# Inverting 16-row triangular blocks: row-by-row substitution against 4x4 blocks joined to 8 and to 16 rows, in the delta-rule stage of a one-core Trainium2 kernel

## The reference, cut to what matters

```python
def step(M, kvq):
    k_t, v_t, q_t = kvq
    out_t = jnp.einsum('bhdk,bhk->bhd', M, q_t)
    kn = k_t / (jnp.linalg.norm(k_t, axis=-1, keepdims=True) + 1e-06)
    pred = jnp.einsum('bhdk,bhk->bhd', M, kn)
    surprise = pred - v_t
    coef = pred + lr[None, :, None] * surprise
    M_new = M - jnp.einsum('bhd,bhk->bhdk', coef, kn)
    return (M_new, out_t)
M_final, outs = jax.lax.scan(step, M0, (k_s, v_s, q_s))
```

## Time and profile before

| what | value |
|---|---|
| median of 3 runs | 1468.79 us (1467.89 to 1471.7) |
| the profiled execution's own time | 1469.33 us |
| its span, first to last instruction | 1467.5 us |
| what lies around the span | 1.8 us |
| mean granted TensorE clock | 0.936 of full speed |
| instructions on DVE | 2568, of them 960 in the inversion (L1270 and L1274, 480 each) |
| busy time of the inversion on DVE | 144.0 us (L1270) and 113.5 us (L1274) |
| the last step's end | POOL and PE lead the chain of waits with 31% and 34% of the span |

### The profile page before, as it was taken

How to read it: one execution, slowest core, us unless ns; L and a number is a source line. 1 busy time by engine, 2 the same in 40 slices (tenths; PEclk the granted TensorE clock), 3 DMA queues, 4 the chain that set the end, 5 groups by cost and what they waited for, 6 DMA issues and landing times.

```text
span 1467.5 us, 45643 instructions
## 1 busy us (share of the span) xinstructions
PE 1253.4 (85%) x17572; PEld 1019.9 (69%) x17572; DVE 870.9 (59%) x2568; ACT 625.4 (43%) x1539; POOL 596.7 (41%) x721
## 2 busy tenths in 40 slices
PE   3889999999994779889888988898889888988764
PEld 3756666666663668778777877787778777877763
DVE  0163433333333377768777777677767777777661
ACT  0012222222221455555555655555555555555431
POOL 0000000000002474566566656665666566556521
PEclk9989999999995789999999999999999999999886
DMA  8769999999940011111111111111111111111110
GB/s 308 266 229 384 374 366 380 376 368 376 375 156 17 3 26 19 30 25 28 23 29 24 27 24 30 24 27 24 29 24 27 23 29 26 25 21 26 24 18 17
DMA packets 176413, 169.84 MB, mean 116 GB/s; under 512 B 118198, under 2 KB 146425, under 8 KB 175609
## 3 DMA queue, kind: packets, MB, share of 16 engines
q1 hardware_dynamic: 176234, 167.37, 35.0%
HBM read 154.72 MB, written 12.58 MB: 114 GB/s over the span
## 4 chain that ended last, share of the span: by engine, by line
PE 34%; POOL 31%; issue 22%; DVE 8%; ACT 2%; DMA 1%; SPq 1%; POOLq 0%; DVEq 0%; ACTq 0%
PE PS L434 29%; POOL region L1092 11%; POOL region L1073 4%; POOL region L1078 3%; POOL xr_lo L1097 2%; POOL region L1086 2%; POOL region L1049 1%; POOL region L1084 1%; PE PS L503 1%; POOL region L1068 1%; POOL region L1063 1%; POOL region L1056 1%; PE PS L673 1%; POOL region L1040 1%; DVE region L1410 1%
## 5 line engine op out<-in xcount | busy, mean ns | idle before, releaser
L434 PE MATMUL PS<-region 64*64 64x64 f32 (+5 forms) x5936 | 366.5, 287 | 44.5 <-DMA region<-in_w 23.0
L434 PEld LDWEIGHTS PS<-region 64*64 64x64 f32 (+3 forms) x5936 | 243.9, 140 | 144.2 <-issue 102.8
L1092 POOL TENSOR_TENSOR region<-region,powers 128x24 f32<-128x24 f32 x64 | 215.2, 3362 | 5.0
L1019 POOL TENSOR_TENSOR region<-region,powers 128x1 f32<-128x1 f32 x32 | 6.1, 189 | 417.1 <-DVE region L1200 417.1
L1280 DVE TENSOR_REDUCE region<-region 128x12 f32<-128x768 f32 x96 | 91.0, 948 | 129.7 <-ACT region L894 129.5
L683 PE MATMUL PS<-region 64*64 64x64 f32 x4608 | 165.1, 228 | 2.4 <-ACT region L922 2.1
L683 PEld LDWEIGHTS PS<-region 64*64 64x64 f32 x4608 | 151.9, 142 | 21.2 <-issue 17.3
L1270 DVE TENSOR_TENSOR region<-region 96x1 f32<-96x1 f32 (+14 forms) x480 | 144.0, 300 | 24.9 <-DMA region<-n_scratch 10.3
L434 PE MATMUL PS<-cw_hi,xr_hi 128*128 128x512 f32 (+3 forms) x384 | 146.8, 382 | 10.0 <-POOL xr_lo L1097 10.0
L434 PE MATMUL PS<-cw_lo,xr_hi 128*128 128x512 f32 (+3 forms) x384 | 138.9, 362 | 0.0
L434 PE MATMUL PS<-cw_hi,xr_lo 128*128 128x512 f32 (+3 forms) x384 | 137.5, 358 | 0.0
(11 more groups left out here) (165 smaller groups left out, 2179.8 us busy)
## 6 DMA issues: line engine op xcount, KB each, us to landing
region<-in_Wq SPq DMA_DIRECT2D x32, 1152.0 KB, 5.6
region<-in_Wk SPq DMA_DIRECT2D x32, 1152.0 KB, 8.0
region<-in_Wv SPq DMA_DIRECT2D x32, 1152.0 KB, 7.6
region<-in_x SPq DMA_DIRECT2D x32, 384.0 KB, 6.6
region<-in_w SPq DMA_DIRECT2D x3, 2304.0 KB, 11.8
region<-h_scratch SPq DMA_DIRECT2D x64, 96.0 KB, 1.9
n_scratch<-region SPq DMA_DIRECT2D x256, 12.0 KB, 1.6
region<-i_scratch SPq DMA_DIRECT2D x256, 12.0 KB, 1.8
```

Of the source, the lines that this page charges most:

```text
L434: return nc.tensor.matmul(dst, lhsT, rhs, start=first, stop=last)
L1092: pool.tensor_tensor(rs[:, cols], rs_var[:, cols], root[:, cols], ALU.pow).then_inc(S["rs_ready"], 1)
```

## The change: what it does

The 16x16 blocks are inverted in three levels instead of row by row. `invert_small` does rows 1 to 3 of all four 4x4 diagonal blocks of each 16x16 block together, with the same multiply and reduce, on access patterns with one more dimension (three multiplies and three reduces). `join(k, 4, 3)` makes two 8x8 inverses out of four 4x4 ones: two multiplies of 64 elements, one reduce of 128 elements to 32 (into the new buffer `mid`), two multiplies of 64, two reduces of 64 to 16. `join(k, 8, 5)` makes the 16x16 inverse out of two 8x8 ones: a multiply of 512 elements, a reduce of 512 to 64, a multiply of 512, a reduce of 512 to 64. The second multiply of each join reads `inv` down its columns: neighbouring elements of that operand lie 16 words apart. Between dependent instructions a semaphore wait stands as before.

In DVE's order `invert_small` and the join of 4 stand where rows 1 to 7 stood, and the join of 8 stands where rows 8 to 15 stood. `prod` grows from 256 to 512 elements a partition and `mid` adds 64. The new function `invert(k)` at the end of the first hunk of code is called by nothing.

```diff
--- before.py
+++ after.py
@@ -246,7 +246,8 @@
         dT = part("second", P, HEADS, SEQ)
         blocks = part("second", NBLK * HEADS, BLK, BLK)
         inv = part("second", NBLK * HEADS, BLK, BLK)
-        prod = part("second", NBLK * HEADS, BLK, BLK)
+        prod = part("second", NBLK * HEADS, 512)
+        mid = part("second", NBLK * HEADS, 64)
         eT = part("second", P, HEADS, SEQ)
         y, c1, z, c = [part("second", P, KD) for _ in range(4)]
         outT = part("second", P, HH, P)
@@ -1259,20 +1260,56 @@
                 dve.tensor_tensor(wo[:, :, :], wo[:, :, :], lr[:, HEADS:].unsqueeze(2).to_broadcast([P, HH, ATT]), ALU.mult)\
                    .then_inc(S["fold_ready"], 1)
 
-            def invert(k, rows):
-
-                if rows[0] == 1:
-                    dve.wait_ge(S["gather_done"], (k + 1) * 16)
-                    need(dve, "inv_stored", k * 16)
-                for r in rows:
+            def diag(buf, at, *dims):
+
+                return bass.AP(buf.tensor, buf.offset + at, [buf.ap[0]] + [list(n) for n in dims])
+
+            def invert_small(k):
+
+                dve.wait_ge(S["gather_done"], (k + 1) * 16)
+                need(dve, "inv_stored", k * 16)
+                for r in range(1, 4):
                     if r > 1:
-                        dve.wait_ge(S["sub_step"], k * (BLK - 2) + r - 1)
-                    dve.tensor_tensor(prod[:, 0:r, 0:r], inv[:, 0:r, 0:r],
-                                      blocks[:, r, 0:r].unsqueeze(1).to_broadcast([NBLK * HEADS, r, r]), ALU.mult)\
-                       .then_inc(S["sub_mul"], 1)
-                    dve.wait_ge(S["sub_mul"], k * (BLK - 1) + r)
-                    last = dve.tensor_reduce(inv[:, 0:r, r], prod[:, 0:r, 0:r], AX, ALU.add)
-                    last.then_inc(S["sub_step" if r < BLK - 1 else "d_ready"], 1)
+                        dve.wait_ge(S["sub_step"], 6 * k + r - 1)
+                    step = BLK * 4 + 4
+                    dve.tensor_tensor(diag(prod, 0, (r * r, 4), (r, r), (1, r)), diag(inv, 0, (step, 4), (BLK, r), (1, r)),
+                                      diag(blocks, r * BLK, (step, 4), (0, r), (1, r)), ALU.mult).then_inc(S["sub_mul"], 1)
+                    dve.wait_ge(S["sub_mul"], 7 * k + r)
+                    dve.tensor_reduce(diag(inv, r, (step, 4), (BLK, r)), diag(prod, 0, (r * r, 4), (r, r), (1, r)), AX, ALU.add)\
+                       .then_inc(S["sub_step"], 1)
+
+            def join(k, size, done):
+
+                pairs = BLK // (2 * size)
+                low = size * BLK
+                step = 2 * (low + size)
+                plane = size * size
+                cube = (plane, size), (size, size), (1, size)
+                dve.wait_ge(S["sub_step"], 6 * k + done)
+                for p in range(pairs):
+                    last = dve.tensor_tensor(diag(prod, p * plane * size, *cube),
+                                             diag(blocks, p * step + low, (0, size), (BLK, size), (1, size)),
+                                             diag(inv, p * step, (BLK, size), (0, size), (1, size)), ALU.mult)
+                last.then_inc(S["sub_mul"], 1)
+                dve.wait_ge(S["sub_mul"], 7 * k + done + 1)
+                dve.tensor_reduce(diag(mid, 0, (1, pairs * plane)), diag(prod, 0, (size, pairs * plane), (1, size)),
+                                  AX, ALU.add).then_inc(S["sub_step"], 1)
+                dve.wait_ge(S["sub_step"], 6 * k + done + 1)
+                for p in range(pairs):
+                    last = dve.tensor_tensor(diag(prod, p * plane * size, *cube),
+                                             diag(mid, p * plane, (size, size), (0, size), (1, size)),
+                                             diag(inv, p * step + low + size, (0, size), (1, size), (BLK, size)), ALU.mult)
+                last.then_inc(S["sub_mul"], 1)
+                dve.wait_ge(S["sub_mul"], 7 * k + done + 2)
+                for p in range(pairs):
+                    last = dve.tensor_reduce(diag(inv, p * step + size, (BLK, size), (1, size)),
+                                             diag(prod, p * plane * size, *cube), AX, ALU.add)
+                return last
+
+            def invert(k):
+                invert_small(k)
+                join(k, 4, 3).then_inc(S["sub_step"], 1)
+                join(k, 8, 5).then_inc(S["d_ready"], 1)
 
             def moments(t, m):
                 dve.wait_ge(S["sq_ready"], 3 * t + m + 1)
@@ -1420,7 +1457,7 @@
                 if live(m):
                     ffn_out(m)
                 if live(k):
-                    invert(k, range(8, BLK))
+                    join(k, 8, 5).then_inc(S["d_ready"], 1)
                 if live(l):
                     gate_and_add(l)
                 if live(x + 1):
@@ -1459,7 +1496,8 @@
                 if live(x + 1):
                     normalise(x + 1)
                 if live(j):
-                    invert(j, range(1, 8))
+                    invert_small(j)
+                    join(j, 4, 3).then_inc(S["sub_step"], 1)
                 if live(t):
                     scale(t, 2)
```

## The result

The changed kernel takes 1401.74 us (median of 4 runs, 1393.09 to 1409.35) against 1468.34 us (4 runs) of the kernel before, a ratio of 0.9534 with a 95% interval of 0.9501 to 0.9567. That is 67 us less; the forecast was 1407 us, 62 us less. The profiled execution took 1401.61 us for a span of 1399.8 us.

A forecast was written before the change was run, and what follows sets the result against it. The prediction took DVE's 29.04 us loop through take_norm as the bound, not PE; 2.37 - 0.5 + 0.07 = 1.94 us a period over 31 periods, plus 1.9 us at the end, gave 1407 us, 8-in-10 range 1382 to 1434 us.

The forecast's parts named there:

- The bound: DVE's loop from take_norm to take_norm, 29.04 us, sets the period, with all of the inversion, 9.09 us, on it.
- The second half: Rows 8 to 15: four instructions in 2.80 us against 5.17, saving 2.37 us a tile before the column cost.
- The column reads: Second multiply of each join, hopping 16 words: 1.0 ns an element, 0.5 us in the second half, 0.13 in the first.
- the row L1147: Existing six-element instruction with two streams hopping 193 words, read as 1.4 ns an element and used to price column reads.
- The first half: Rows 1 to 7, 14 instructions become 13: 0.07 us saved a period, between -0.5 and +0.5.
- two meetings with L1097: POOL's L1097 starting 1.55 or 1.20 us into the first half: ends at 3.4 (0.5 saved) or 3.7 us (0.1 lost).
- The sum: A period: 2.37 - 0.5 + 0.07 = 1.94 us saved, 29.04 to 27.10; 62 us in all, 1407 us.
- the rival with free columns: Joins' column reads cost nothing: 2.57 us a period, 1387 us; chance 0.15, shared with a better meeting with L1097.
- Dear columns: Joins' column reads cost 1.4 to 2.8 ns an element: 1416 to 1444 us; chance 0.14 (beyond 1425).
- Short runs: Joins' runs of 4 and 8 elements cost 8 ns each: period 0.5 us longer, 1485 us; chance 0.04 (slower).
- PE taking over: PE's loop, 25.4 us, 27.2 with lower clock, bounds: 1411 us, or 1468; chance 0.05 that it or another wait takes nearly all.
- fixed to `take_norm`: The gather's load and its landing before the inversion keep their time behind take_norm, so neither saving touches them.

The follow-up runs named there:

- e5: Changed kernel with take_norm moved up on DVE behind gate_and_add, norm_h2 moved back, and key_lengths ahead of residual_rstd on POOL: 1369.21 us, ratio 0.9359.
- e1: First half of the change alone, rows 8 to 15 one by one as in the kernel before: 1463.75 us, ratio 0.9964, commonest period 28.55 us.
- e3: Changed kernel with the second multiply of both joins reading inv along rows, so the result isn't the inverse: 1378.49 us, ratio 0.9385.
- e2: Changed kernel with both 8x8 diagonal blocks by substitution, two at once, then the join of 8: 1409.13 us, ratio 0.9587.
- e6: Changed kernel with right_side and high_part moved ahead of moments(t, 2), into DVE's wait for ACT: 1387.35 us, ratio 0.9472.
- e4: Changed kernel, same inverse, with the joins' second multiply reading rows and the reduce after it reading prod with a hop: 1400.52 us, ratio 0.9526.
- e8: Changed kernel with GpSimd's low_part (L1098) cut to 128x64 elements from the second tile on, so the output is another: 1365.72 us, ratio 0.9317.
- e9: Changed kernel with the moves of e5 and e6 together: 1366.39 us, ratio 0.9312.
- e10: e9 with POOL's low_part also moved ahead of input_rstds: 1350.53 us, ratio 0.9188.
- e7: Changed kernel with PE's gates(x) placed ahead of start_y(k), in its wait for take_e: 1395.41 us, ratio 0.9504.

## Why the prediction was right, point by point

*The bound.* Right in the main: the period repeats through `take_norm` (e5), and the second half of the inversion lies on the loop whole (e1, e3). After the change every stretch but the two halves kept its length (11.71, 4.48, 1.13, 2.64). But the sentence that all 30 instructions of the inversion lie on the loop is too broad. The stretch from `take_norm` through `take_e`, `start_y`, ACT's squares and DVE to the join of 4 has POOL's way to L1098 beside it, and POOL's ends last (e2, e6): of the first half only what is left behind L1098's end counts. The forecast's own sum for the first half had this right, since it let L1097 keep its time behind `take_norm`.

*The second half.* Forecast 2.80 us and 0.5 for the columns, 3.30; measured 3.12. The interpolated 699 and 682 ns were 677 and 682. The column reads were over-priced: 0.377 us instead of 0.5, as the row L1147, with its two hopping streams, gave too much for one. The estimate from the Trainium skill, "Vector Engine (DVE) Microarchitecture Reference", section 5.2 (0.35 to 0.74 us), holds the measured value at its lower end. e3 shows that the order of the words makes the difference; that pairs of adjacent words are what counts, as the page has it, no run here shows. e4 bears on a remark there, that a one-source read alternating between two regions ran at full rate: a reduce reading with a constant hop of 8 words didn't.

*The first half.* The forecast worked out two meetings with L1097, with ends at 3.4 and 3.7 us, and took a value between them less 0.13 for columns. Both were measured, 3.43 and 3.77; the commonest is the better one, 0.49 us saved where I took 0.07.

*The sum.* The two terms together were under-sized: the commonest period fell by 2.54 us, not 1.94, 0.60 us or 19 us over 31 periods. That the time came out within 5 us of the forecast all the same is luck: the mean lies 0.49 us above the commonest period (15 us over 31), against 0.07 before, and no step of mine had this term. With all periods at 26.50 the time would have been about 1387 us, the value of the rival with free columns, though the columns aren't free. Part of the term is the clock: the seven falls behind `start_y` hold 10.0 of the 15.2 us. But falls at this place are in seven periods of the kernel before as well, and those exceed 29.04 by only 2.9 us together. What differs most is the meeting with L1098. Before, a late start of the inversion made the first half shorter: in the seven periods DVE's wait for ACT's squares is 4.8 us longer in sum, and the halves are 2.4 us shorter (3.55 to 3.70 us each in place of 3.92). After, the wait is 6.8 us longer and six of the seven halves are 3.76 to 3.78 us in place of 3.43, 2.0 us longer in sum. In four more periods, with no fall, the inversion starts only 0.2 to 0.3 us late, and each is about 0.6 us longer. With a short L1098 (e8) the half never exceeds 2.83 us.

*The rivals.* Free columns: out, by the 1054 ns. Dear columns: out, 0.74 ns an element is below 1.4. Short runs: 677 ns for 64 runs of 8 leaves nothing for a run. PE taking over: in one inner period of the changed kernel (from 857.93, 26.87 us, with a fall of the clock `take_norm` starts 0.04 us after PE's key norms), not in the others; but its loop of 25.4 us, worked out for it, is what e5, e9 and e10 stop at (25.45). The gather isn't fixed to `take_norm`, as the forecast called it: its blocks land 15.0 to 16.9 us after it in the inner periods of e6, against the 16.19 at which the changed kernel needs them, and one period there (from 667.13, 28.04 us) waited 1.10 us for them.

## What to carry to other kernels

Find the loop that repeats and add up its stretches until they give the period; a change that lies on it whole can then be priced closely (e1's 28.55 us). But look for a second way between the same two points: here POOL's ended later than the one that was added up, and what was done ahead of its end was covered (e2, e6). Where a waiting instruction stands in an in-order queue can be worth nearly half as much as making it faster (e5). For small dependent vector instructions count instructions and waits, not elements. When a period's commonest value and its mean differ, forecast both: what happens only in some periods took back 15 of some 82 us here.

## What the runs showed of the hardware that was not expected

A DVE multiply with both inputs in SBUF that is issued while GpSimd's 128x512 subtraction runs waits to the end of it (1.19 us for a pair that takes 0.44 in e8 and 0.45 in e10), while a reduce issued in the same stretch ran its usual 0.28 us. Not every GpSimd instruction does this: DVE multiplies with both inputs in SBUF took 0.15 to 0.19 us while L1093, which works on 128x12 elements for 2.34 us, ran. A hop at every element costs a two-input multiply 0.72 to 0.74 ns an element at 16 words and a reduce 0.89 ns at 8 words. TensorE's clock fell to its lower level behind waits of 1.5 to 1.6 us at `start_y` in some periods and not in others with the same wait; with that wait filled (e7) it fell in none of the 29 inner periods.
